# Residual and results loaded in pieces between the groups' loads, and a round's eight row scatters issued in its last three slots

## The reference

```
x = x + _L0_attn_ref(_layernorm(x), ...)       # a selective state-space mixer: conv, 16 states per channel, scan over 256 steps
x = x + _L0_xattn_ref(_layernorm(x), ctx, ...) # cross attention, 16 heads over 64 keys, masked
x = x + _L0_ffn_ref(_layernorm(x), ...)        # mixture of experts: 8 experts, the best 2 of each token, hidden size 512
...
gate_scores = softmax(x @ Wg + bg)
h = relu(x @ W1[e] + b1[e]);  expert_out = h @ W2[e] + b2[e]
topk_scores, topk_idx = top_k(gate_scores, 2);  top_probs = softmax(topk_scores)
out = sum(expert_out[topk_idx] * top_probs)
```

## Time and profile before

| | |
|---|---|
| median of three runs | 1040.76 us |
| profiled execution, its own time | 1042.74 us |
| its span in the trace | 1040.9 us |
| mean granted clock of TensorE | 0.865 |
| PE, DVE, POOL busy, share of the span | 76%, 71%, 68% |

### The profile page before, as it was taken

One profiled execution on the slowest core, in us unless ns is written; L12 is line 12 of the kernel. 1 busy time (PEld: TensorE's weight loads), 2 busy tenths in 40 slices (PEclk: granted clock), 3 DMA queues, 4 the chain that ended last, 5 costly groups with the idle time before them and its releaser, 6 DMA issues. The chain is left out here.

```text
span 1040.9 us, 12598 instructions
## 1 busy us (share of the span) xinstructions
PE 787.0 (76%) x3871; PEld 498.4 (48%) x3871; DVE 744.2 (71%) x1060; ACT 488.9 (47%) x1086; POOL 704.4 (68%) x501
## 2 busy tenths in 40 slices
PE   5667677797778778867877886774768998799592
PEld 1233343363344345334524542452446688798592
DVE  3279987989996897899789889958952625233172
ACT  3557456557475545746564674434213334232130
POOL 0159987978699779878977996787661445554252
PEclk9888788998899679878976997776688999999797
DMA  2324382282264228225522642385016446867872
GB/s 67 126 101 147 125 246 95 93 214 84 91 179 139 84 96 225 90 91 149 167 84 83 190 127 75 121 202 162 1 37 194 132 116 178 255 187 196 270 215 79
DMA packets 111076, 143.51 MB, mean 138 GB/s; under 512 B 18392, under 2 KB 83557, under 8 KB 111008
## 3 DMA queue, kind: packets, MB, share of 16 engines
q1 hardware_dynamic: 106016, 134.26, 43.9%
q0 software_dynamic: 4992, 8.45, 2.5%
HBM read 110.48 MB, written 34.01 MB: 139 GB/s over the span
## 5 line engine op out<-in xcount | busy, mean ns | idle before, releaser
L1185 POOL TENSOR_TENSOR prod<-hst,BC 128x1024 f32<-128x1024 f32 x128 | 303.9, 2374 | 121.6 <-DVE hst L1332 120.3
L1332 DVE TENSOR_TENSOR_SCAN hst<-dA,Rp 128x1024 f32<-128x1024 f32 x128 | 292.6, 2286 | 12.2 <-DVE Rp L1323 0.4
L993 ACT ACTIVATE dA<-dtm,Aneg 128x255 f32<-128x255 f32 x512 | 216.0, 495 | 146.4 <-DVE hst L1332 146.2
L571 PE MATMUL Y<-prod,ident 128*128 128x256 f32 x512 | 167.7, 461 | 65.0 <-POOL prod L1190 58.6
L1266 POOL DMA_INDIRECT y2d<-prod,BC x92 | 90.6, 984 | 136.6 <-DVE prod L1627 114.9
L571 PEld LDWEIGHTS Y<-prod,ident 128*128 128x128 f32 x512 | 108.5, 225 | 140.7 <-POOL prod L1190 93.8
L1190 POOL TENSOR_TENSOR prod<-prod 128x512 f32<-128x512 f32 x128 | 163.6, 1278 | 10.0
L1323 DVE TENSOR_TENSOR Rp<-BC,Rp 128x1024 f32<-128x1024 f32 x128 | 156.5, 1223 | 5.5 <-DMA BC<-bcd 1.5
L571 PE MATMUL Rp<-BC,prod 128*128 128x128 f32 x736 | 92.0, 279 | 8.2 <-DVE prod L1627 8.2
L571 PE MATMUL T<-Kbd,qT 64*128 64x512 f32 x128 | 62.5, 862 | 45.9 <-DVE mx L1376 45.9
L571 PEld LDWEIGHTS Rp<-BC,prod 128*128 128x128 f32 x736 | 90.5, 195 | 13.3 <-issue 10.8
(11 more groups left out here) (222 smaller groups left out, 1255.7 us busy)
## 6 DMA issues: line engine op xcount, KB each, us to landing
BC<-bcd SPq DMA_DIRECT2D x64, 1024.0 KB, 5.4
BC<-in_L_ffn_W SPq DMA_DIRECT2D x92, 256.0 KB
xsd<-blank SPq DMA_DIRECT2D x18, 1032.0 KB, 13.8
BC<-xsd SPq DMA_DIRECT2D x46, 129.0 KB
soft<-in_L_ffn_b SPq DMA_DIRECT2D x46, 64.0 KB
xin<-in_x SPq DMA_DIRECT2D x8, 256.0 KB, 4.1
x2d<-x2o SPq DMA_DIRECT2D x8, 256.0 KB
E<-x2d SPq DMA_DIRECT2D x1, 2048.0 KB
```

The costliest lines, as they stand in the source:

```text
L571: return pe.matmul(o, l, r_, start=start, stop=stop, **kw)
L993: m = A(dA[:, k % RING, i, 1:SEQ], dtm[:, r % 2, d, b * SEQ + 1:(b + 1) * SEQ], ACT.Exp, scale=Aneg[:, d, c * NC + i:c * NC + i + 1])
L1185: TT(prod[:, k % RING, :, :], hst[:, k % RING, :, :], BC[:, (k // 2) % BCR, 1, :, :], ALU.mult).then_inc(s_pd, 1)
L1332: v.tensor_tensor_scan(hst[:, k % RING].rearrange("p n s -> p (n s)"), dA[:, k % RING].rearrange("p n s -> p (n s)"), U.rearrange("p n s - ...
```

## The change

Three things are different. First, a round's eight scatters all stand in slots 13 to 15: two, three and three. `tail2` goes, and with it the five extra slots at the end of `LASTS`. This holds for every round, as the code of POOL's `slot` has no case for a single one. Second, the residual is loaded in four pieces of 512 KB, behind the loads of groups 21, 24, 27 and 30, each with a semaphore of its own. Third, the six loads of results stand one by one behind the loads of groups 36 to 41.

```diff
-        LASTS = 2 * STEPS + 5
+        LASTS = 2 * STEPS
...
-            def load_results(i):
+            def load_results(i, c):
                 n = ROUNDS * NTT // FINAL
-                for c in range(2):
-                    src = y2d[c * ROWS:(c + 1) * ROWS, :].rearrange("(p t) d -> p t d", p=P)[:, i * n:(i + 1) * n, :]
-                    sp.dma_start(ys[c][:, i * n:(i + 1) * n, :], src).then_inc(s_e[i], 16)
+                src = y2d[c * ROWS:(c + 1) * ROWS, :].rearrange("(p t) d -> p t d", p=P)[:, i * n:(i + 1) * n, :]
+                sp.dma_start(ys[c][:, i * n:(i + 1) * n, :], src).then_inc(s_e[i], 16)
+
+            def load_residual(i):
+                n = ROUNDS // FINAL
+                if i == 0:
+                    sp.wait_ge(Tp.sem, Tp.at("o", ROUNDS - 1))
+                sp.wait_ge(s_x2, 16 * n * (i + 1))
+                sp.dma_start(acc[:, i * n * NTT:(i + 1) * n * NTT, :].rearrange("p (r t) c -> p r (t c)", t=NTT),
+                             x2d[i * n:(i + 1) * n, :, :, :].rearrange("r p t c -> p r (t c)")).then_inc(s_acc[i], 16)
...
                     store_x2(ROUNDS - 1)
-                    sp.wait_ge(s_x2, 16 * ROUNDS)
-                    sp.wait_ge(Tp.sem, Tp.at("o", ROUNDS - 1))
-                    sp.dma_start(acc.rearrange("p (r t) c -> p r (t c)", t=NTT), x2d[:, :, :, :].rearrange("r p t c -> p r (t c)")).then_inc(s_acc, 16)
+                if j > 3 * WR and j % 3 == 0 and j // 3 - WR <= FINAL:
+                    load_residual(j // 3 - WR - 1)
...
-                if j == PARTS[1].group + WR - 1:
+                n = j - PARTS[1].group - WR + 1
+                if n == 0:
                     scattered(PARTS[1].group)
-                    for i in range(early):
-                        load_results(i)
+                if 0 <= n < 2 * early:
+                    load_results(*divmod(n, 2))
...
-                if tail2 and k < 2 * NTT - 3:
-                    scatter(r - 3, k + 3)
                 if tail:
                     if k == 9:
                         row_ids(r - 2)
                     if k >= STEPS - 3:
-                        scatter(r - 2, k - STEPS + 3)
+                        for n in ((0, 1), (2, 3, 4), (5, 6, 7))[k - STEPS + 3]:
+                            scatter(r - 2, n)
...
                 if c == 0:
                     v.wait_ge(s_e[i], 32)
+                    v.wait_ge(s_acc[i], 16)
...
                     weights()
-                    v.wait_ge(s_acc, 16)
```

More of the change, by code:

```diff
@@ L332, in decoder @@
         s_ys = sem("s_ys")
-        s_acc = sem("s_acc")
+        s_acc = [sem(f"s_acc{i}") for i in range(FINAL)]
         s_y = [sem(f"s_y{i}") for i in range(YR)]
@@ L409, in behind @@
         def behind(r):
-            return 1 <= r <= ROUNDS, 2 <= r <= ROUNDS + 1, 3 <= r <= ROUNDS + 2
+            return 1 <= r <= ROUNDS, 2 <= r <= ROUNDS + 1
         TRIO = ((0, 1), (4, 5)), ((2, 3), (6, 7))
@@ L561, in _ @@
             for i in range(early, FINAL):
-                load_results(i)
+                for c in range(2):
+                    load_results(i, c)
             for i in range(early, FINAL):
@@ L759, in slot @@
                 ln, nxt = ahead(r)
-                prev, tail, tail2 = behind(r)
+                prev, tail = behind(r)
                 if tail:
```

## The result

The changed kernel took 1064.85 us (median of 4 runs, 1060.79 to 1069.07) against 1041.03 us for the kernel before (4 runs, 1035.5 to 1041.91). The ratio is 1.0241, 95% interval 1.0185 to 1.0296: it is slower, by 23.8 us between the medians, 1.9 to 3.0 per cent, where +7.5 had been forecast. The forecast range ended at 1063, so the time lies outside it. The profiled execution of the changed kernel took 1060.79 us, the fastest of the four; its span is 1058.9 us, 18.0 more than the 1040.9 before. Helper lines have moved by 7 or 8 (L571 is L579, L1217 is L1225, L1266 is L1273, L1627 is L1634).

The account below looks back on a forecast made before the run. DVE bounds the first phase, held up in slot 4 by POOL's place; PE nearly fills the second. 16.2 − 1.6 − 4 + 2.0 − 4.7 = +7.9 us on 1042.74 (1.98 above the median), forecast 1048.5 us, range 1033 to 1063.

Parts of the forecast that it names:

- Part 1: Round starts 3 to 7, first phase: scatters ahead of POOL's gate cost 3.1 us four times, 3.8 once, +16.2.
- Part 2: Start of the groups: the last scatter of round 5 starts earlier against the scan, −1.6 us.
- Part 3: Second phase: residual in pieces, rounds 6 and 7's scatters beside groups; −4 us, plus 2.0 for three more DMAs.
- Part 4: Second phase: results in pieces, rows of group 45 land at 1008.4 against 1013.11, −4.7 us.
- the rival on the clock: PE's granted clock falls in each slot 2, convolution 3.0 to 3.6 us longer four times, +14, 1062.5; chance 0.22.
- long rows of scatters: Second phase: five scatters ahead of a `tile_back` hold DVE's `tile_out`; no −4 but 2, twice: 1054 us; chance 0.05.

Follow-up runs that it names:

- the run of this part alone: Against the kernel before. Under Part 1: only scatters of rounds 0 to 5 moved, 1054.94 us against 1042.35; under Part 4: only results in pieces, 1038.04 against 1042.35.
- round 5 alone: Kernel before with only round 5's scatters moved to slots 13 to 15, and residual and results loaded in pieces: 1036.16 us against 1043.64.
- the loads alone: Kernel before with only residual and results loaded in pieces, all scatters as before: 1037.18 us against 1042.35, ratio 0.9946.

## Why the prediction was wrong

**Part 1, its path right, its size a little too large, what was to show it not seen.** The step by step sum for the start of a round (four scatters ahead of the fold of step 1, then 3.60 us of convolution, then the logits) gave +4.6 us for the logits and +3.1 for x1T; the trace has 4.57 and 2.75. Round 7 was to lose 3.8 and lost 3.44. In all 14.3 for 16.2, and the run of this part alone confirms it with +12.6, part 2 included (16.2 − 1.6 = 14.6 had been predicted). The starts of rounds 3 to 6 lost 2.5 to 2.8 us each, of 3.1. The signs did not come as written: the idle time before the logits and x1T was to grow by about 3 us and fell from 4.73 to 4.07, and PE was to wait 3 us before the convolution and waited 0.45. The sum left out the second way, from the fold of step 15 over the scores and `oT`, which holds DVE 3.33 us one slot earlier and was as long as the first to within 0.45 us. That the size came out even so is in part luck.

**Part 2, right.** 1.6 predicted; 14.3 − 12.6 = 1.7 in the trace, and 1.4 at the first load in the trace with round 5 alone (776.66 for 778.02). Between the medians of that kernel (−7.5) and of the loads alone (−5.2) it is 2.3, which these runs can't tell from nothing.

**Part 3, wrong, and this is the step that failed.** "I take the middle, −4", with 2.0 for three more DMAs, and nothing in the sum for the longer rows of scatters. Up to the load of group 36 the groups lost 12.1 us instead of gaining 2. The −4 and the missing term both failed. The stalls of PE beside groups 14 to 16 that the −4 was to win back are not the residual's, since 5.15 us of them are there before any residual is issued. And the rows cost what the sum had at nothing: 9.7 us between the loads of groups 11 and 12, and 8.86 − 4.94 = 3.9 at round 7's. I had read the row that mattered: DVE's `tile_out` at 833.36 and 893.61 ended behind a row of scatters and not with the residual. I took it as a bound on the gain, and priced longer rows at "2, twice" in a rival with a chance of 0.05. What I missed is that the hold lengthens itself. A held `tile_out` no longer parts POOL's rows, twelve DMAs stand without a break in the trace, and DVE and ScalarE both stop, PE with them for 10.40 us.

**Part 4, right, a little too small.** −4.7 predicted for `tile_in` of group 45. From load 36 to the end 6.7 us were gained in the profile, 4.3 by the run of this part alone; the kernel before has the longest such stretch of all kernels with the six loads together (77.9 us, the others 74.9 to 76.9), so the 6.7 flatter. PE's wait before `tile_in` of group 37 is 2.52 us where 2 had been expected, and SP's loads of groups 37 to 41 come 4.34 to 5.61 us apart, for 4.8.

**The rivals.** The time lies beside that of the rival on the clock (1062.5), but by chance. A wait of 3 us with half the clock behind it did come, but at the sum of step 15 and not at the convolution: that still takes 3.60 us and starts behind a wait of 0.45. It cost some 1.7 us (2.07 for 1.03 in the sum, 1.77 for 1.13 in the scores behind it) on a way that wasn't longer than the other for it, and the mean granted clock is 0.874 where it was 0.865. The rival that happened is the one on long rows of scatters. It had the right places and too small a price: 2 us for PE's 10.40 at the first and for 3.9 more at the second. (With its "no −4 but 2, twice" the sum is 1056.6 and not the 1054 that stands there.)

## What to carry to other kernels

Before several indexed DMAs are put together, look in the trace at what the shortest row of them does to the other engines, and ask what ends the row. If the row ends only when a held engine goes on, a longer row closes up with the next. Ahead of an operation that another engine waits for, nearly every us of instructions on the queue counts. Moved behind it the same instructions cost less, but not nothing: 12.6 us lost one way and 12.7 gained the other look alike, while in a steady round it was 2.7 lost and 0.5 to 0.9 gained. So compare stretches of the trace and not only the end. And the parts of a change are to be timed apart, since here 7 us of gain lay hidden in 23 of loss.

## What the runs showed of the hardware

While POOL issues indexed DMAs in a row, one every 1.27 us, DVE and ScalarE start late. DVE goes on 0.7 to 2.4 us after the end of the row's last DMA, after waits of up to 9.71 us, or before that end or right at it, after 6.4 to 7.9 us of waiting (6.38 and 7.82 in the traces above). ScalarE, where it is held too, goes on within 0.1 us of it in the changed kernel's row of twelve. Each instruction that was held so is one that waits for a signal of PE, whose rows had ended by then, while DVE's own signal reached POOL within the row: the held `tile_out` ended at 849.01, and the `tile_back` that waits for it started at 850.33. SP's DMAs came 1.4 us apart instead of 0.5. Whether it is PE's signal that comes late or the waiting engine that doesn't see it stays open, and so does whether POOL's issuing does it or the transfers that it starts: no run parts them. The long hold was there in four traces with 0.3 to 1.3 us between two rows and not in three with 2.0 to 2.3; why the same instructions leave now the one and now the other is open too.

After a wait of 2.98 us PE's four matmuls of a sum took 2.07 us instead of 1.03, at a granted clock of 0.50, and the convolution 12 us later took its old 3.60.
